# Layer 2 of a four-layer GNN kernel: gathers of 128 rows in place of 125

## The reference

```python
z = jnp.einsum('nd,hdf->nhf', h, W)
es = jnp.einsum('nhf,hf->nh', z, a_src)
ed = jnp.einsum('nhf,hf->nh', z, a_dst)
e = jax.nn.leaky_relu(es[src] + ed[dst], SLOPE)
e = jnp.where(e == 0.0, NEG, e)
m = jax.ops.segment_max(e, dst, num_segments=N)
...
ex = jnp.exp(e - m[dst])
denom = jax.ops.segment_sum(ex, dst, num_segments=N)
...
out = jax.ops.segment_sum(alpha[:, :, None] * z[src], dst, num_segments=N)
```

## Time and profile before

| | |
|---|---|
| median of three runs | 2123.56 us (2113.93 to 2126.78) |
| profiled execution, its own time | 2130.72 us |
| its span | 2128.9 us |
| TensorE clock granted, mean | 0.81 |
| busy: PE, PE weight loads | 1889.9 us, 1653.3 us |
| busy: DVE, POOL, ACT | 1282.8 us, 732.5 us, 447.1 us |
| L445, the 425 gathers | 572.7 us busy on POOL |

### The profile page before, as it was taken

One profiled execution on the slowest core, in us unless ns is written; L12 is line 12 of the kernel. 1 busy time (PEld: TensorE's weight loads), 2 busy tenths in 40 slices (PEclk: granted clock), 3 DMA queues, 4 the chain that ended last, 5 costly groups with the idle time before them and its releaser, 6 DMA issues.

```text
span 2128.9 us, 38284 instructions
## 1 busy us (share of the span) xinstructions
PE 1889.9 (89%) x13533; PEld 1653.3 (78%) x13533; DVE 1282.8 (60%) x2915; ACT 447.1 (21%) x1000; POOL 732.5 (34%) x567
## 2 busy tenths in 40 slices
PE   6679999999999999999389788898777887899998
PEld 5468888888888788888278777787776784588887
DVE  9577677777777421212388878888877876411111
ACT  0421222122212100100223222332223224300000
POOL 0112222222222200001488888888888850000000
PEclk9989999999999999999655555555655555699999
DMA  6111111111121434443233333333333322044441
GB/s 175 49 57 73 66 65 80 80 66 65 65 96 66 186 114 155 143 159 106 53 84 86 81 81 86 85 86 83 81 78 79 84 57 93 32 167 167 167 167 42
DMA packets 110199, 202.38 MB, mean 95 GB/s; under 512 B 70372, under 2 KB 87061, under 8 KB 100483
## 3 DMA queue, kind: packets, MB, share of 16 engines
q1 hardware_dynamic: 54851, 141.62, 18.8%
q0 software_dynamic: 55232, 59.15, 11.5%
HBM read 152.00 MB, written 53.36 MB: 96 GB/s over the span
## 4 chain that ended last, share of the span: by engine, by line
PE 72%; POOL 8%; issue 7%; DVE 5%; DMA 4%; ACT 3%; DVEq 0%; SPq 0%; another core or an unknown queue 0%; POOLq 0%; ACTq 0%
PE bank L1219 25%; PE bank L1155 10%; PE bank L1163 10%; PE bank L1285 10%; POOL ring L445 8%; PE bank L1152 4%; DMA ring<-attention_rows,work 2%; PE bank L1276 2%; PE bank L1181 2%; PE bank L1349 2%; DMA work<-in_src 1%; PE bank L1259 1%; PE bank L1227 1%; PE bank L1172 1%; PE bank L1332 1%
## 5 line engine op out<-in xcount | busy, mean ns | idle before, releaser
L445 POOL DMA_INDIRECT ring<-attention_rows,work x425 | 572.7, 1348 | 154.9 <-issue 144.6
L1285 PE MATMUL bank<-work,ring 125*65 125x48 f32 x3400 | 395.9, 303 | 0.0
L1285 PEld LDWEIGHTS bank<-work,ring 125*65 125x65 f32 x3400 | 388.4, 225 | 8.3
L1155 PE MATMUL bank<-work 128*128 128x100 bf16 x2400 | 304.1, 273 | 0.0
L1219 PE MATMUL bank<-big,ring 128*128 128x256 f32 x1250 | 273.0, 379 | 1.4 <-DVE x_sb L816 1.4
L1219 PE MATMUL bank<-big 128*128 128x256 f32 x1250 | 272.9, 379 | 0.0
L1219 PEld LDWEIGHTS bank<-big,ring 128*128 128x128 f32 x1250 | 236.5, 190 | 33.8 <-DVE x_sb L816 2.2
L1219 PEld LDWEIGHTS bank<-big 128*128 128x128 f32 x1250 | 236.6, 190 | 31.7
L1155 PEld LDWEIGHTS bank<-work 128*128 128x128 bf16 x2400 | 242.6, 117 | 0.0
L1163 PE MATMUL bank<-big 128*128 128x256 bf16 x1875 | 213.9, 276 | 14.6 <-ACT big L488 14.6
L1152 PE MATMUL bank<-work 128*128 128x100 bf16 x800 | 218.3, 273 | 7.0 <-DVE work L778 4.6
(11 more groups left out here) (204 smaller groups left out, 2180.8 us busy)
## 6 DMA issues: line engine op xcount, KB each, us to landing
adjacency<-big SPq DMA_DIRECT2D x25, 1600.0 KB, 5.2
ring<-adjacency SPq DMA_DIRECT2D x25, 1600.0 KB, 7.0
big<-adjacency SPq DMA_DIRECT2D x25, 1600.0 KB, 6.9
ring<-attention_rows,work POOLq DMA_INDIRECT x425
edge_rows<-edge_list SPq DMA_DIRECT2D x1, 4983.0 KB
x_sb<-in_x SPq DMA_DIRECT2D x1, 3072.0 KB
out_x<-xnT SPq DMA_DIRECT2D x24, 128.0 KB, 4.3
attention_rows<-ring SPq DMA_DIRECT2D x13, 135.0 KB, 2.2
```

The lines of the kernel that those rows point to most:

```text
L445: G.indirect_dma_start(out=rows[0:EP, s, c, 0:ZG], out_offset=None, in_=ztab[:, :], in_offset=bass.IndirectOffsetOnAxis(ap=idx[:, s, c:c + ...
L1155: ins = mm(w_banks[b][:, 0:NT * QUAD * PAN].rearrange("p (b d) -> p b d", b=NT)[:, :, cols], lo[:, g, :, k], wtd[:, j, g, :, k].rearrange( ...
L1285: ins = mm(sum_banks[three(s)][0:FH, h * WIN:(h + 1) * WIN], rows[0:EP, s, c, h * FH:(h + 1) * FH], prob[:, s % 2, c, h * WIN:(h + 1) * WI ...
```

## The change

EP becomes 128. E = 53125 is no multiple of 128 x 25, so there are now 83 full groups of 640 edges, one with 5 edges (REST = 1 partition of 5) and one without any: GROUPS stays 85, because it is rounded up to a multiple of the five slots. The source numbers are copied from DRAM to a longer DRAM table `source_nodes`, whose last 1275 places are filled with 0 from a small tile. Destinations of the padding are 1e30 in `dstf`, which equal no node of a window, so those edges add nothing. The lowest node of an empty group is cut to N, and the highest is taken over the real edges alone. Everything whose shape has EP grows from 125 to 128 partitions, or from 125 to 128 columns.

Lines in the changed kernel stand 15 (SP's and POOL's layer 2), 17 or 20 (DVE and PE) further down. The diff:

```diff
--- before.py
+++ after.py
@@ -39,8 +39,12 @@
     N, D = x.shape
     E = src.shape[0]
     H, _, F = w_att.shape
-    EP = max(p for p in range(1, P + 1) if E % (p * KC * SLOTS) == 0)
-    GROUPS = E // (EP * KC)
+    EP = P
+    FULL = E // (EP * KC)
+    GROUPS = -(-E // (EP * KC * SLOTS)) * SLOTS
+    REST = (E - FULL * EP * KC) // KC
+    SPARE = GROUPS * EP * KC - E
+    SPK = max(k for k in range(1, 65) if SPARE % k == 0)
     TURNS = GROUPS // SLOTS
     NT = -(-N // P)
     NPAD = NT * P
@@ -50,6 +54,7 @@
     TAIL = E - (P - 1) * COLS
     CGRP = COLS // GRAN
     MOST = -(-ROWS // (P // GRAN)) + 1
+    assert FULL * EP * KC + REST * KC == E and 0 < REST < EP and 0 < SPARE and SPARE // SPK <= P
     assert TURNS > 2 and SLOTS % 2 and NPAD - N >= WIN and D == 2 * P
     assert 0 < TAIL <= COLS - GRAN and DEAD * GRAN + P <= P * COLS + GRAN and N < NOWHERE and NT * PAN <= 128 and DLO * DHI >= N and DB * HALF == COLS
     FH = F + 1
@@ -71,6 +76,7 @@
         flat = nc.dram_tensor("edge_list", (P * COLS + GRAN, FIELDS), BF16, kind="Internal").ap()
         etab = nc.dram_tensor("edge_rows", (ROWS + 1, P * FIELDS), BF16, kind="Internal").ap()
         atab = nc.dram_tensor("adjacency", (NT, P, AT), F32, kind="Internal").ap()
+        src_all = nc.dram_tensor("source_nodes", (GROUPS * EP * KC,), I32, kind="Internal").ap()
         ztab = nc.dram_tensor("attention_rows", (NPAD, ZG), F32, kind="Internal").ap()
 
         iota_w = sb("iota_w", [P, WIN])
@@ -169,7 +175,9 @@
         dlo = carve(P, COLS, dt=BF16)
         dhi = carve(P, COLS, dt=BF16)
         tab = carve(P, COLS, FIELDS, dt=BF16)
-        dst_i = carve(EP, GROUPS, KC, dt=I32)
+        dst_i = carve(EP, FULL + 1, KC, dt=I32)
+        within = carve(EP, GROUPS, KC)
+        spare = carve(SPARE // SPK, SPK, dt=I32)
 
         ybuf = big2[:, 0:2 * NPAD].rearrange("p (t f) -> p t f", f=D)
         aw = [big2[:, (2 + j) * NPAD:(3 + j) * NPAD].rearrange("p (b d) -> p b d", b=NT) for j in range(2)]
@@ -233,6 +241,7 @@
         s_digits, s_dup = sem("s_digits"), sem("s_dup")
         s_gq, s_hist, s_histc, s_hT, s_colsum, s_colsumc, s_first, s_cur, s_nswb = (
             sem(f"s_{n}") for n in ("gq", "hist", "histc", "hT", "colsum", "colsumc", "first", "cur", "nswb"))
+        s_srcs = sem("s_srcs")
         s_tab, s_flat, s_etab = sem("s_tab"), sem("s_flat"), sem("s_etab")
         s_gm, s_gmT, s_dg, s_bb, s_sweeps = (sem(f"s_{n}") for n in ("gm", "gmT", "dg", "bb", "sweeps"))
         s_onehots, s_cnt, s_deg, s_sqd, s_dinv = (sem(f"s_{n}") for n in ("onehots", "cnt", "deg", "sqd", "dinv"))
@@ -302,7 +311,12 @@
             sp.dma_start(att_b[:], att.partition_broadcast(P)).then_inc(ld_wts, 16)
             for j, b in enumerate((b0, b_rel, b3)):
                 sp.dma_start(bias[:, j, :], b.partition_broadcast(P)).then_inc(ld_wts, 16)
-            sp.dma_start(dst_i[:], dst.rearrange("(g p k) -> p g k", p=EP, k=KC)).then_inc(ld_dsti, 16)
+            sp.dma_start(dst_i[:, 0:FULL, :], dst[0:FULL * EP * KC].rearrange("(g p k) -> p g k", p=EP, k=KC)).then_inc(
+                ld_dsti, 16)
+            sp.dma_start(dst_i[0:REST, FULL, :], dst[FULL * EP * KC:E].rearrange("(p k) -> p k", k=KC)).then_inc(ld_dsti, 16)
+            sp.dma_start(src_all[0:E].rearrange("(a e) -> a e", a=GROUPS), src.rearrange("(a e) -> a e", a=GROUPS)).then_inc(
+                s_srcs, 16)
+            sp.dma_start(src_all[E:E + SPARE].rearrange("(p k) -> p k", k=SPK), spare).then_inc(s_srcs, 16)
 
             sp.wait_ge(s_tab, 6)
             sp.dma_start(flat[0:P * COLS, :].rearrange("(p e) f -> p e f", p=P), tab[:]).then_inc(s_flat, 16)
@@ -345,7 +359,8 @@
 
             sp.wait_ge(s_sweeps, 1)
             nsw = sp.value_load(nsw_i[0:1, 0:1], min_val=1, max_val=SWEEPS)
-            src_v = src.rearrange("(g p k) -> p g k", p=EP, k=KC)
+            sp.wait_ge(s_srcs, 32)
+            src_v = src_all.rearrange("(g p k) -> p g k", p=EP, k=KC)
             with sp.Fori(0, nsw) as r:
                 sp.wait_ge(y["based"], r + 1)
                 sp.sem_inc(held, 1)
@@ -615,7 +630,9 @@
             V.memset(x_sb[:, NT - 1, :], 0.0)
             V.memset(dst_e[96:P, :], NOWHERE)
             V.memset(src_e[96:P, :], 0)
+            V.memset(spare, 0)
             V.memset(w_e[96:P, :], 0.0).then_inc(s_pad, 1)
+            link(V.memset(dstf[:, FULL:, :], BIG))
             V.memset(epsc[:], EPS)
             V.memset(far[:], -3 * BIG)
             V.memset(ones[:], 1.0)
@@ -717,10 +734,13 @@
                 V.tensor_copy(w_rr[:, :, (1 - m) * D:(2 - m) * D],
                               banks[2 + m][:, :].rearrange("p (k o) -> p k o", k=2)).then_inc(s_wTc, 1)
 
-            dve.wait_ge(ld_dsti, 16)
-            link(V.tensor_copy(dstf[:], dst_i[:]))
+            dve.wait_ge(ld_dsti, 32)
+            V.tensor_copy(dstf[:, 0:FULL, :], dst_i[:, 0:FULL, :])
+            link(V.tensor_copy(dstf[0:REST, FULL, :], dst_i[0:REST, FULL, :]))
             V.tensor_reduce(gmin[:], dstf[:], AX_X, ALU.min)
-            V.tensor_reduce(gmax[:], dstf[:], AX_X, ALU.max).then_inc(s_gm, 1)
+            link(V.scalar_tensor_tensor(out=within, in0=dstf[:], scalar=BIG / 2, in1=dstf[:], op0=ALU.is_lt, op1=ALU.mult))
+            link(V.tensor_scalar(gmin[:], gmin[:], float(N), None, ALU.min))
+            V.tensor_reduce(gmax[:], within, AX_X, ALU.max).then_inc(s_gm, 1)
             dve.wait_ge(s_gmT, 1)
             V.tensor_reduce(cmin[:], banks[6][0:GROUPS, 0:EP], AX_X, ALU.min)
             link(V.tensor_reduce(cmax[:], banks[6][0:GROUPS, EP:2 * EP], AX_X, ALU.max))
```

## The result

The changed kernel took 2177.9 us (median of four runs, 2173.1 to 2181.3) against 2125.1 us of the kernel before (2113.9 to 2126.8): ratio 1.0258, 95% interval 1.0217 to 1.0299. The forecast, 2097 us with a range of 2060 to 2126, was wrong on these runs, and on the wrong side. At the end of the experiments the same kernel, not a character of it changed, was run again and took 2098.0 us (2089.8 to 2105.1, six runs), ratio 0.9901 (0.9863 to 0.9940). Both results stand. What lies between them is a stall that the first profile shows and the second does not: the two profiled executions differ by 90.2 us in their spans, 88.9 of it in the attention loop.

A forecast was written before the change was run, and what follows sets the result against it. POOL's gathers were taken to bound the attention loop, with a PE-and-DVE loop 0.6 us a group behind. Attention loop -32.3, its start -3.2, steps before +1.6: -33.9 from the profiled 2130.7 gives 2097 us, range 2060 to 2126.

The forecast's parts named there:

- POOL falls behind the 7.87 us loop: Layer 2 attention loop: POOL, at 7.2 us a group, stops being the bound and the PE-and-DVE loop sets the pace.
- All turns become short ones: Attention loop: every turn of five groups takes the short kind's pace, 7.87 us a group after corrections, saving 32.3 us.
- a spare POOL: Sign in the attention loop: POOL should wait for in-DRAM indices once a group.
- Case 5: Attention loop gathers: each participating engine costs POOL time, 1334 ns a gather, +0.63 us a group, 2184 us; chance 0.05.
- Price of a gather: POOL's gather in the attention loop: 989 ns instead of 1211, at 13 ns a row on the fullest engine.
- Stretching: POOL's gathers in the attention loop: mean above median adds 0.7 us a group, making 7.2 us.
- The PE-and-DVE loop: Attention loop: the second bound, 0.6 us a group behind POOL, would pace it at 7.87 us, clock staying low.
- collides: DVE L922 in the attention loop, stretched by a gather, costs 0.31 us; half, 0.15 us a group, taken off.
- The sum: Whole kernel: -32.3 - 3.2 + 1.6 = -33.9 us against the profiled 2130.7 us, so 2097 us.
- Start and prologue: Attention loop's start: -3.2 us from ten faster gathers and a shorter landing; steps before it: +1.6 us.
- Case 2: Attention loop: POOL drops behind and the clock rises too, 7.5 us a group, 2066 us; chance 0.10.

The follow-up runs named there:

- after_again: The changed kernel with nothing edited, run again on chip 1 as a control: 2098.0 us, ratio 0.9901.
- gather65: The changed kernel with each gather fetching only the first 65 partitions, the other rows left out: 2108.4 us, ratio 0.9904.
- ep126: The changed kernel with 126 partitions in a group instead of 128, on chip 4: 2194.1 us, ratio 1.0331.
- half_rows: The changed kernel gathering 128 rows from a copy of the first 135 columns, half of each row left out: 2108.7 us, ratio 0.9894.
- gather128_again: gather128_only with nothing edited, run again on chip 1 as a control: 2088.4 us, ratio 0.9852.
- gather128_only: The kernel before with each gather fetching 128 rows instead of 125, groups still 625 edges, on chip 4: 2199.0 us, ratio 1.0355.
- pause_between: The changed kernel with a memset on POOL after each gather and a wait for it, on chip 4: 2365.9 us, ratio 1.1132.
- gap2: The changed kernel with two one-column memsets on POOL ahead of every gather, without a wait between them: 2102.1 us, ratio 0.9867.

## Why the prediction failed, and what of it held

**The step that failed** is the one of the attention loop: "POOL falls behind the 7.87 us loop", after which "All turns become short ones" and 84 intervals take 661.1 us. They took 746.9. 17 intervals with a stall stand in place of short ones, and each stall also lets POOL run through all its slots, so that most of POOL's 110.9 us of waiting for indices (28.2 in after_again) is the stall's effect and not the sign of a spare POOL that I had named. What sets the stall off stays open. Case 5 gave 2184 us and lay near the time, but its mechanism was not there: it wanted gathers of 1334 ns, and they took 947. No case had an engine other than POOL and DVE held up by the gathers. Nothing in the trace of before had pointed there but 14 late increments in 358, at five places (near 1187, 1297, 1467, 1516 and 1651 us); I had not looked for them.

Where there is no stall, each term can be held against after_again. Its gathers, the packets of 1305 to 1345 us, and L942:

```profile
L460 POOL DMA_INDIRECT ring<-attention_rows,work x425: 942/946/2567, 1035.4 to 1694.5; - x142
...
  DVE work L933: 57.2, 21
```

```profile
L460 POOL DMA_INDIRECT ring<-attention_rows,work x425 | 530.9, 1249 | 154.9 <-issue 126.7 <-DMA work<-source_nodes 28.2
```

```profile
L942 DVE TENSOR_SCALAR work<-work x85: 159/165/323, 1043.9 to 1701.5; 128x20 f32<-128x20 f32 x85
```

1. **Price of a gather:** 989 ns forecast, 946 measured, 48 packets. Right, slightly too dear. I had priced single rows of the fullest engine, at 13 ns. The runs point at rows taken by fours, the last four started included: 911 to 926 ns for one four, 945 to 947 for two (gather65 with 5 rows on an engine, the changed kernel with 8), 997 for three (ep126, 9 rows), 1211 for seven (25 rows). From two fours on, each further one costs some 53 ns, and 5 rows cost what 8 do. half_rows fits too: 8 rows of half the bytes, 947 ns.
2. **Stretching:** I carried over 0.7 us a group. It is 5 x (1249 - 946) ns = 1.5 us. Less than half of it foreseen. Five gathers and their pauses come to 7.7 us a group, so POOL does not drop behind: DVE L933 still waits for it 57.2 us in 21 groups.
3. **The PE-and-DVE loop:** 7.87 us forecast, 7.41 measured, at the same low clock:

```profile
1242.12:1249.53 7.41, 6.86 (x54) 6.05 (x54) 6.67 (x19) 1.82 (x5) 5.89 (x6) 0.50 0.34 91
```

   L942 no longer collides (median 165 ns, had 394), but that was not worth 0.31 us: from L1288 to L972 the loop takes 1.44 us and took 1.42. L972 has 0.35 us for 0.40 and its successor follows sooner, 0.09 us in all. The rest, 0.37 us, is in L1259, of which I had no row and which I let grow with its columns. Before and after_again, L1259 and L1279, least/median/most ns:

```profile
L1259 PEld LDWEIGHTS bank<-work x425: 129/227/227, 1036.0 to 1735.1; 48*125 48x125 bf16 x142
```

```profile
L1279 PEld LDWEIGHTS bank<-work x425: 92/101/116, 1036.5 to 1695.3; 48*128 48x128 bf16 x142
```

   A bf16 weight load of 125 columns takes 227 ns at the low clock (129 at least, at the high one), one of 128 takes 101. Five loads with their matmuls took 0.69 us and take 0.30. With 126 columns (ep126) it is 227 ns still. The Trainium skill (TensorE: Matmul & The Clock Gate, the section on weight-path modes) has the rule that I missed: fast weight load is on when there are 128 weights and the type is not f32. By that rule, the trace agrees at 125, 126 and 128. The intervals agree too: those that occur most are 7.4 us in after_again and 7.8 in gather128_again, whose groups are still 125 wide.
4. **All turns short:** no. 52 of 84 intervals are under 7.6 us, 16 lie between 8.9 and 10.2. One of these:

```profile
1385.53 2.50 POOL L460 DMA_INDIRECT ring<-attention_rows,work  x1 [0.30 <-issue]
1385.77 1.14 DVE L992 TENSOR_TENSOR work<-work 128x960 f32<-128x960 f32 x1
...
1386.97 0.24 DVE L997 TENSOR_SCALAR big<-work 128x192 f32 x1
1388.34 0.94 POOL L460 DMA_INDIRECT ring<-attention_rows,work  x1 [0.30 <-issue]
...
1390.07 0.18 DVE L933 TENSOR_TENSOR work<-ring,work 128x20 f32<-128x20 f32 x1 [2.85 <-DMA ring<-attention_rows,work]
```

   The gather starts just ahead of L992 and takes 2.50 us in place of 0.95; L933 idles 2.85 us for it. 16 of the 84 intervals are of this length, near 9.5 us, and give back part of what the faster loop gained. gather128_again, whose loop takes 7.8 us, has none; why the loops fall against each other so at 7.4 and not at 7.8 was not tested. The Trainium skill (GPSIMD Engine Reference, Specifications) says that POOL's access to SBUF contends with DVE instructions that have two inputs there. L992 is one, and the trace agrees for it: the 82 gathers in whose first 0.95 us it runs for 0.2 us or more take, at the median, 1.54 us more than a gather usually does. But L953 has the same size and two such inputs as well, and costs the 95 gathers that it meets in this way only 0.16 us, so that the size does not follow from the rule.
5. **The sum:** first and last L972 of after_again are

```profile
1050.46 0.35 DVE L972 TENSOR_TENSOR work<-ident,work 96x192 f32<-96x192 f32 x1
...
1708.47 0.35 DVE L972 TENSOR_TENSOR work<-ident,work 96x192 f32<-96x192 f32 x1
```

   658.0 us for 84 intervals; forecast 661.1. 40 intervals are near 7.4 us, 16 near 9.5, 12 near 8.0 (nearly all the last of a turn), 4 near 7.8, and 12 are 6.3 to 6.9 us, at a granted clock of 0.78 on the mean; before had one as short. Misses of opposite sign, a loop 0.46 us shorter and short intervals at a higher clock against a POOL that still stretches, nearly cancel.
6. **Start and prologue:** from the first gather to the first L972 15.1 us, before 19.1: -4.0 for -3.2. The first gather comes 0.4 us later, for +1.6.

The forecast was summed against a profiled execution, and its like is the profiled execution of after_again: 2130.7 - 35.4 - 4.0 + 0.4 = 2091.7 us by the measured terms, 2091.1 measured, 6 us under the forecast. That 2097 and the median 2098.0 agree is thus partly luck. Case 2, the clock, played a part: between the first and the last of these lines the granted clock was 0.53 before and 0.58 in after_again, against the 0.52 that I had expected to stay.

**Is the rest of the change worth anything?** gather128_again, in the same batch as after_again, took 2088.4 us (2087.3 to 2089.4) against 2098.0 (2089.8 to 2105.1). In it POOL has left the chain of waits (share of the span), while in after_again it has a larger share than the 8% of before. after_again, then gather128_again:

```profile
PE 66%; POOL 15%; issue 8%; DVE 5%; ACT 3%; DMA 2%; DVEq 0%; POOLq 0%; SPq 0%; ACTq 0%
```

```profile
PE 84%; DVE 7%; issue 3%; ACT 3%; DVEq 1%; POOL 0%; DMA 0%; SPq 0%; ACTq 0%; POOLq 0%
```

Widening the gather alone, with the groups left at 625 edges and no copied table, brings all of the gain and some 10 us more on chip 1. On chip 15 it ran only with small additions (2087.0 and 2089.0 us), and the changed kernel likewise (2084.6 to 2098.4), so there the order of the two is not shown. On chip 4 it is the slowest but one. Until that stall is understood, neither can be recommended.

## What to carry to other kernels

Run the unedited kernel once more beside every batch of experiments, before you believe that an edit mended it: I held the kernel before fixed in each batch, which never showed the stall, and so took a change of chip, or of what went with it, for the effect of five idle instructions. Price an operation that gets a new shape from a row of that shape, and not by growing it with its columns; 125 to 128 columns here made a load twice as fast. And when a faster engine removes a wait, ask which phase the two loops will fall into, since the same two loops gave turns of 39.9 or 43.5 us.

## What the runs showed of the hardware

- A software gather's time follows the number of fours of rows on its fullest DMA engine, the last four started included. For 32, 65, 128, 126 and 125 rows, spread by the packets over 16, 13, 16, 14 and 5 engines, these are one, two, two, three and seven fours, and the median times 926, 945, 946, 997 and 1211 ns. Halving the bytes of a row left 947 (half_rows).
- In the runs on chip 4, and in none on chips 1 and 15, PE's semaphore increments came 1 to 3 us late, now and then more (up to 8.8 us in the first profile of the changed kernel, of unknown chip), while gathers of 126 or 128 rows followed one another at 1.25 to 1.30 us. Between 1070 and 1770 us PE, DVE, ACT and SP stood still together for 67 us in gather128_only (5 in the kernel before, 0 in gather128_again), counting pauses of 0.6 us or more in which none of the four starts anything. What is held, and by what, is open.
- A wait of POOL for its own last memset cost 0.81 us (pause_between); two memsets without a wait between two gathers cost nothing (gap2).
- bf16 weight loads, mostly at the low clock: 227 ns at the median with 125 or 126 columns, 101 with 128.
- A gather that meets DVE L992 takes 1.54 us more at the median, one that meets L953, of the same size, 0.16 us more (after_again).
